# An embedding stage with four word buffers, normalized rows in PSUM and the text stores queued ahead of the expert weights' loads

## The chip, the cores and the metric

The kernel runs on one core of a Trainium2 chip. The metric is the device time of one execution in microseconds (us). TensorE (PE), VectorE (DVE), ScalarE (ACT), GpSimd (POOL) and SyncE (SP, which only issues transfers here) run side by side; each takes its instructions in order, and they wait for one another and for the DMA transfers by semaphores.

## What is computed

An early-fusion transformer block of depth 1, in float32. 64 images of 3 x 64 x 64 become 16 patches each, and 64 texts of 77 tokens become 77 rows each; together 64 x 93 = 5952 tokens of width 192. Attention and a product-key expert layer follow, with a residual around each.

```
tok:  patches(x) @ W.T + b                                 # 64 x 16 rows of 192
txt:  e = W_word[x_txt] + W_pos[pos] + W_type[..] + W_match_tok[..] + W_match_ent[..]
          + W_sf_tok[..] + W_sf_ent[..] + W_etype[..] + W_atype_ent[..]
      (e - mean(e)) * rsqrt(var(e) + 1e-12) * gamma + beta # 64 x 77 rows of 192
h = concat(tok, txt)                                       # per sample 93 rows
attn: w = h' @ w_qkv; softmax over the tokens of |w|^2 per head; out @ w_out + b_out
ffn:  z = x @ P; scores = z . C; top 4 of 64 in each of 8 groups;
      gelu(z W1[i]) W2[i] for the chosen ones, weighted; gelu(comb G1) G2
```

The change touches only the first two (`tok` and `txt`) and when the expert weights W2 are loaded.

## The kernel before

**Three stages.** The embedding stage writes all 5952 rows to a scratch tensor in DRAM (`h0`). The attention stage takes 16 units of 4 samples, and loads each unit's rows from it (`x0`). The expert stage takes 12 tiles of 496 tokens and holds nearly all of the time. One SBUF tensor (`arena`) is carved up anew for each stage, so the attention stage's tiles lie on the embedding stage's. `stage1_over` is the wait that separates them: all text and image stores landed (`s_todma`, `s_idma`), the three bfloat16 parts of w1 made (`s_ws`), b2 and w2 placed in their padded tiles (`s_bc`, `s_w2c`). Every engine executes it.

**Text rows.** The 4928 text rows are taken in 11 groups (`JJ`), each four tiles of 112 rows (16 samples x 7 positions). For group jj:

- GpSimd (`gather`) waits until the sum of group jj-2 is taken (`s_emb`), copies four columns of word ids to `wnow`, waits for the copy, and issues four indirect DMAs that fetch 112 rows of `W_word` each into `word[:, par]`, one of two buffers.
- VectorE (`onehots`) makes one-hot matrices of the position ids and the small tables' ids; TensorE (`tables`) multiplies them with the tables: 16 matmuls into PSUM (`pair0` or `pair1`).
- VectorE (`text_step(jj)`), in this order: one-hots of group jj+1; the sum of PSUM and word rows (`emb`, line 1166); `scaled(jj-1)` (line 1140); the statistics of jj (1173); `shifted(jj-1)` (1148), which adds beta and writes `tout`, one of two output buffers, after the stores of jj-3 have landed; moments of jj (1179) and the negated mean (1182).
- GpSimd (`text_rstd`, lines 691 and 693) makes the reciprocal deviation, ScalarE (`mean_off`, line 861) takes the mean off: from `emb` to `tnorm`, two SBUF buffers. `scaled` multiplies `tnorm` with deviation and gamma into `tmul`, in SBUF.
- SP (`store_text`, line 538) issues four stores of 16 x 7 rows each.

**Image rows.** TensorE (`image(k)`, 8 times 14 matmuls, lines 1515 and 1517) works on the patches `xt`, a load of 3 MB, into PSUM banks 4 and 5. ScalarE copies and stores them. In TensorE's order, tables of groups 0 and 1 come first, then twice `image` and once `tables`, four times, and the tables of groups 6 to 10 last.

**Expert weights.** W2 is loaded by 32 DMAs of 32 KB (line 549) into `w2f`, which lies on the patches' tile; so they wait for the last image matmul (`s_ips`). On SP they stand between `store_text(2)` and `store_text(3)`. W1 comes in one load of 1 MB that ScalarE issues (line 889) behind group 3. ScalarE casts it behind `mean_off(7)`; VectorE makes the rest (lines 1202 and 1205) between groups 8 and 9. ScalarE copies w2 to its place (line 905) behind `mean_off(8)`, and issues DMAs of the w1 parts (`stack_part`, line 873, 512 KB each) behind `mean_off` of groups 8, 9 and 10.

## Time and profile before

| | |
|---|---|
| median of 3 runs | 1409.76 us (1407.14 to 1412.56) |
| the profiled execution's own time | 1408.9 us |
| its span | 1406.8 us |
| busy, share of the span | PE 88%, DVE 78%, ACT 78%, POOL 72% |
| chain that ended last, first lines | ACT L1068 19%, ACT L1080 9%, POOL L821 5%, PE L1741 5%, PE L1728 4%, DVE L1476 4% |
| bytes moved | 107.05 MB |

The span is that of the instructions in the trace; 2.1 us lie around it. The chain's lines are those of the expert tiles (gelu, gates, the two products of each expert). The row format is: engine, line, operation, output<-input, and after it in brackets the idle time of the engine just before, with what ended it. "SPq" and "ACTq" are rows for DMA issues. An idle time that names a DMA ended when that transfer landed; where the engine named had long been done, it was another that came last.

### The profile page before, as it was taken

How to read it: one execution, taken by the hardware profiler on the slowest of the kernel's cores; microseconds unless marked ns; L12 is line 12 of the kernel's file. 1: busy time of each engine (PE TensorE's matmuls, PEld its weight loads, DVE VectorE, ACT ScalarE, POOL GpSimd, SP SyncE). 2: the span in 40 equal slices, each digit the busy share in tenths (PEclk: the TensorE clock that was granted, in tenths of full speed). 3: DMA queues.
4: the chain of work that ended last, by engine and by line, in shares of the span. 5: the costliest groups of instructions: out<-in, count | busy, mean ns of one | idle time of the engine just before them, and what ended most of it. 6: DMA issues, size and time to landing. Idle time of an engine off the chain costs nothing.

```text
span 1406.8 us, 34237 instructions
## 1 busy us (share of the span) xinstructions
PE 1237.8 (88%) x12232; PEld 622.3 (44%) x12232; DVE 1101.4 (78%) x3359; ACT 1093.7 (78%) x2708; POOL 1015.5 (72%) x735
## 2 busy tenths in 40 slices
PE   4742799999999999858999999999999999999996
PEld 3741466666666666533333333333333333333332
DVE  5574378888888888866888888888878888888883
ACT  0232557677767776538999999999999999999994
POOL 6661356775677567626888988888798888879894
PEclk8965799999999999968999999999999999999997
DMA  9644312322232222133224232222413322231410
GB/s 273 141 113 85 63 33 73 99 65 68 74 98 65 68 74 89 55 84 102 55 52 94 56 78 63 56 68 55 100 38 81 75 59 64 56 87 44 91 38 12
DMA packets 95704, 107.05 MB, mean 76 GB/s; under 512 B 12772, under 2 KB 92668, under 8 KB 95254
## 3 DMA queue, kind: packets, MB, share of 16 engines
q1 hardware_dynamic: 91184, 96.00, 26.5%
q10 hardware_dynamic: 2240, 5.08, 2.2%
q0 software_dynamic: 2112, 3.79, 1.1%
q8 instruction: 98, 1.61, 0.5%
q14 instruction: 70, 0.57, 0.1%
HBM read 67.88 MB, written 33.71 MB: 72 GB/s over the span
## 4 chain that ended last, share of the span: by engine, by line
ACT 29%; PE 11%; POOL 7%; DVE 4%; issue 4%; POOLq 0%; DVEq 0%; ACTq 0%
ACT ring L1068 19%; ACT arena L1080 9%; POOL arena L821 5%; PE code L1741 5%; PE ring L1728 4%; DVE arena L1476 4%; PE ring L1760 2%; POOL arena L829 1%; POOL arena L827 1%; ACT arena L1076 0%; ACT arena L1088 0%; PE ring L1751 0%; POOLq L157 0%; PE ring L1578 0%; PE ring L1626 0%
## 5 line engine op out<-in xcount | busy, mean ns | idle before, releaser
L1476 DVE TENSOR_TENSOR arena<-ring,arena 128x496 f32<-128x496 f32 x1008 | 611.6, 668 | 132.6 <-ACT ring L1068 131.8
L821 POOL TENSOR_TENSOR arena<-arena 128x992 f32<-128x992 f32 x264 | 608.4, 2316 | 113.5 <-ACT arena L1080 103.5
L1068 ACT ACTIVATE ring<-ring 128x496 f32<-128x496 f32 x1008 | 543.8, 689 | 11.8 <-PE ring L1728 10.8
L1728 PE MATMUL ring<-arena,w_stack 99*32 99x496 bf16 x6144 | 428.2, 375 | 25.6 <-DVE arena L1476 19.7
L1741 PE MATMUL code<-arena,w_pad 128*32 128x496 f32 x3072 | 389.0, 580 | 3.6 <-ACT arena L1084 3.3
L1728 PEld LDWEIGHTS ring<-arena,w_stack 99*32 99x32 bf16 x6144 | 159.8, 95 | 414.6 <-DVE arena L1476 252.4
L1080 ACT ACTIVATE arena<-ring 128x992 f32<-128x992 f32 x252 | 282.6, 1121 | 3.5 <-POOL arena L821 2.9
L1570 PE MATMUL ring<-arena 96*128 96x372 f32 x384 | 135.3, 490 | 1.6 <-ACT arena L924 0.9
L1741 PEld LDWEIGHTS code<-arena,w_pad 128*32 128x32 f32 x3072 | 96.6, 110 | 53.4 <-DVE arena L1476 17.8
L757 POOL TENSOR_TENSOR arena<-arena 128x372 f32<-128x372 f32 x96 | 91.9, 986 | 33.2 <-DVE arena L1316 33.2
L1570 PEld LDWEIGHTS ring<-arena 96*128 96x128 f32 x384 | 71.8, 194 | 62.4 <-ACT arena L932 15.8
L1619 PE MATMUL ring<-arena 128*128 128x376 f32 x192 | 78.5, 534 | 21.4 <-DVE arena L1311 15.3
L932 ACT ACTIVATE arena<-ring 128x93 f32<-128x93 f32 x384 | 92.6, 280 | 0.0
L752 POOL TENSOR_TENSOR arena<-arena 124x512 f32<-124x512 f32 x48 | 51.9, 1082 | 50.9 <-DVE arena L1248 50.7
L932 ACT ACTIVATION_READ_ACCUMULATOR arena<-ring 128x1 f32 x384 | 86.5, 239 | 0.0
L1248 DVE MAX8 arena<-arena 124x8 f32<-124x64 f32 x384 | 53.1, 211 | 40.8 <-ACT arena L969 40.8
L770 POOL TENSOR_TENSOR arena<-arena 124x576 f32<-124x576 f32 x16 | 22.4, 1402 | 82.5 <-DVE arena L1372 81.8
L1259 DVE MATCH_REPLACE8 arena<-arena 124x72 f32<-124x72 f32 x384 | 78.3, 216 | 0.0
L765 POOL TENSOR_TENSOR arena<-arena 128x372 f32<-128x372 f32 x96 | 74.7, 807 | 2.1 <-DVE arena L1338 2.1
L930 ACT COPY arena<-ring 128x372 f32<-128x372 f32 x96 | 46.9, 488 | 33.5 <-PE ring L1570 33.5
L1638 PE MATMUL code<-arena 128*124 128x192 f32 x384 | 68.9, 330 | 2.8 <-POOL arena L765 2.8
L918 ACT ACTIVATE arena<-arena 124x192 f32<-124x192 f32 x96 | 45.6, 539 | 33.1 <-DVE arena L1241 33.1
(140 smaller groups left out, 1467.1 us busy)
## 6 DMA issues: line engine op xcount, KB each, us to landing
arena<-gates SPq DMA_DIRECT2D x48, 496.0 KB, 6.7
gates<-arena SPq DMA_DIRECT2D x16, 744.0 KB, 11.5
arena<-h_scratch SPq DMA_DIRECT2D x32, 279.0 KB
arena<-z_parts SPq DMA_DIRECT2D x144, 62.0 KB, 2.7
h_scratch<-arena SPq DMA_DIRECT2D x16, 279.0 KB
z_parts<-arena SPq DMA_DIRECT2D x48, 93.0 KB, 2.1
arena<-h_scratch SPq DMA_DIRECT2D x12, 372.0 KB
out_h<-arena SPq DMA_DIRECT2D x12, 372.0 KB
```

The source lines that it names most:

```text
L757: p_.tensor_tensor(w2pi[:, c], wpi[:, c], wv[:, c], ALU.mult).then_inc(s_w2pi, 1)
L765: p_.tensor_tensor(o, o, natt[:, c].unsqueeze(2).to_broadcast([128, UB, N]), ALU.mult).then_inc(s_o, 1)
L821: p_.tensor_tensor(spaces[quad % SPACES][:, j:j + 2], hid[:, POOL_DUOS.index(duo) % 2], gst[:, block // EB, j:j + 2], ALU.mult).then_inc(s ...
L932: last = a_.activation(wsq[:, c, N * b:N * b + N], src[:, N * b:N * b + N], ACT.Square, accum_out=n2[:, c, b:b + 1])
L1068: a_.activation(product, product, ACT.Gelu_apprx_tanh).then_inc(s_hid, 1)
L1080: a_.activation(to_pool, product, ACT.Gelu_apprx_tanh).then_inc(s_hid, 1)
L1259: last = v_.match_replace(mr[:, s, g], v4[:, s, g], sc[:, s, g], CHOSEN)
L1476: v_.tensor_tensor(spaces[quad % SPACES][:, j + p], duo_bank(duo, p), gst[:, block // EB, j + p], ALU.mult).then_inc(s_gat, 1)
L1570: mm = t_.matmul(o, wq[:, h, 128 * c:128 * c + 128], xT["A"][:, h], start=(h == 0), stop=(h == 1))
L1619: t_.matmul(pair0[:, c % 2, 0:UB * (N + 1)], headsel[:, c], pis.rearrange("p b n -> p (b n)"), start=True, stop=True).then_inc(s_pb, 1)
L1728: mm = t_.matmul(bank[32 * q:32 * q + 32], w1s[:, x + 32 * q:x + 32 * q + 32], zst[:, o, j + p], start=True, stop=True)
L1741: mm = t_.matmul(code_bank[32 * j:32 * j + 32, 0:TN], w2p[:, chunk(2 * j + o, eb, k)], spaces[quad % SPACES][:, j], start=(quad == 0), sto ...
```

## The change

**Words.** There are four word buffers (`word_even`, and `word_odd` in a part of `arena` that the attention stage's small tiles leave free), each with a semaphore. `gather(jj)` waits for the sum of group jj-4 only, and reads its row ids from `widx` itself: `wnow` and its copy are gone. Groups 0 to 3 are gathered at the start.

**Rows in PSUM.** `mean_off` writes to PSUM banks 4 and 5 (`normed`), `scaled` works there in place, `shifted` reads from there. `tnorm` and `tmul` are gone. The row buffer is single: `mean_off(jj)` waits for `shifted(jj-1)`. Images use banks 6 and `code` in place of 4 and 5.

**SP's order.** Stores of groups 0 to 5 come first, then four times eight w2 loads and one group's stores, then the stores of group 10. The first `x0` load waits for stores alone (`stage1_stored`), and what is behind it for the whole of `stage1_over`.

**ScalarE's order.** w2 is placed behind `mean_off(10)`.

The core of the diff:

```diff
+        cw = Carver(cl.at)
+        word_odd = cw(TT, [2, 4, D])
...
+        def word(jj):
+            return (word_even, word_odd)[jj % 2][:, jj // 2 % 2]
+        def normed(rows=TT):
+            return ring[0:rows, 4:6, 0:2 * D]
...
-        def stage1_over(eng):
+        def stage1_stored(eng):
             eng.wait_ge(s_todma[0], 64 * 6)
             eng.wait_ge(s_todma[1], 64 * 5)
             eng.wait_ge(s_idma[0], 16 * 4)
             eng.wait_ge(s_idma[1], 16 * 4)
+        def stage1_over(eng):
+            stage1_stored(eng)
             eng.wait_ge(s_ws, 2)
...
-            store_text(0, 0)
-            store_text(1, 1)
-            store_text(2, 0)
+            for jj in range(6):
+                store_text(jj, jj % 2)
             sp.wait_ge(s_ips, 8)
...
-            for a in range(2):
-                for e in range(EB):
-                    for g in range(EB):
+            for e in range(EB):
+                for a in range(2):
+                    for g in range(EB // 2):
                         rows = slice(64 * a + 16 * e, 64 * a + 16 * e + 16)
-                        sp.dma_start(w2f[rows, g], w2_from[a, e, g]).then_inc(s_w2f, 16)
-            for pr in range(0, 4):
-                store_text(2 * pr + 3, 1)
-                store_text(2 * pr + 4, 0)
-            stage1_over(sp)
+                        sp.dma_start(w2f[rows, 2 * g], w2_from[a, e, 2 * g]).then_inc(s_w2f, 16)
+                        sp.dma_start(w2f[rows, 2 * g + 1], w2_from[a, e, 2 * g + 1]).then_inc(s_w2f, 16)
+                store_text(6 + e, e % 2)
+            store_text(10, 0)
+            stage1_stored(sp)
...
-            for i in range(-2, UNITS + 1):
+            pass_sp(-2)
+            stage1_over(sp)
+            for i in range(-1, UNITS + 1):
                 pass_sp(i)
...
-            def gather(jj, par):
-                wait_apart(pool, (s_emb, jj - 1))
-
-                p_.tensor_copy(wnow[:, par], widx[:, bass.ds(4 * jj, 4)]).then_inc(s_wnow, 1)
-                wait_apart(pool, (s_wnow, jj + 1))
+            def gather(jj):
+                wait(pool, s_emb, jj - 3)
                 for bb in range(4):
+                    x = 4 * jj + bb
                     p_.indirect_dma_start(
-                        word[:, par, bb], None, t["w_word"],
-                        bass.IndirectOffsetOnAxis(ap=wnow[:, par, bb:bb + 1], axis=0)).then_inc(s_word[par], 16)
+                        word(jj)[:, bb], None, t["w_word"],
+                        bass.IndirectOffsetOnAxis(ap=widx[:, x:x + 1], axis=0)).then_inc(s_word[jj % 4], 16)
...
-                a_.copy(img[:, k % 2], banks[k % 2][:, 0:D]).then_inc(s_iev, 1)
+                a_.copy(img[:, k % 2], banks[2 + k % 2][:, 0:D]).then_inc(s_iev, 1)
...
-                wait(act, s_tmul, jj - 1)
+                wait(act, s_to, jj)
                 for bb in range(4):
-                    last = a_.activation(tnorm[:, jj % 2, bb], emb[:, jj % 2, D * bb:D * bb + D], ACT.Identity,
+                    out = normed()[:, bb // 2, D * (bb % 2):D * (bb % 2) + D]
+                    last = a_.activation(out, emb[:, jj % 2, D * bb:D * bb + D], ACT.Identity,
                                          bias=tneg[:, bb:bb + 1])
...
-                if jj == 8:
+                if jj == 10:
                     act.wait_ge(s_w2f, 16 * 2 * EB * EB)
...
-                    last = v_.scalar_tensor_tensor(out=tmul[:, bb], in0=tnorm[:, par, bb], scalar=trs[:, bb:bb + 1],
+                    x = normed()[:, bb // 2, D * (bb % 2):D * (bb % 2) + D]
+                    last = v_.scalar_tensor_tensor(out=x, in0=x, scalar=trs[:, bb:bb + 1],
                                                    in1=tgam, op0=ALU.mult, op1=ALU.mult)
```

GpSimd's order at the start of the program, where L685 is a gather, L682 the copy of ids, and L691 with L693 `text_rstd`. Before:

```order
L682 COPY arena<-arena 112x4 [waits word_ids_loaded]
L685 DMA arena<-in_w_word,arena 112x192 [waits word_indices_placed]
L685 DMA arena<-in_w_word,arena 112x192 x3
L682 COPY arena<-arena 112x4
L685 DMA arena<-in_w_word,arena 112x192 [waits word_indices_placed]
L685 DMA arena<-in_w_word,arena 112x192 x3
L699 AFFINE_SELECT ident<-ident 128x128 [waits constants_zeroed]
L691 TENSOR_SCALAR arena<-arena 112x4 [waits text_moments]
L693 TENSOR_TENSOR arena<-arena 112x4 [waits text_var_eps]
L682 COPY arena<-arena 112x4 [waits emb_summed]
L685 DMA arena<-in_w_word,arena 112x192 [waits word_indices_placed]
```

And now, where L697 is a gather, L703 with L705 `text_rstd`:

```order
L697 DMA arena<-in_w_word,arena 112x192 [waits word_ids_loaded]
L697 DMA arena<-in_w_word,arena 112x192 x15
L711 AFFINE_SELECT ident<-ident 128x128 [waits constants_zeroed]
L703 TENSOR_SCALAR arena<-arena 112x4 [waits text_moments]
L705 TENSOR_TENSOR arena<-arena 112x4 [waits text_var_eps]
L697 DMA arena<-in_w_word,arena 112x192 [waits emb_summed]
```

Sixteen gathers stand ahead of the first `text_rstd` where eight stood.

SP's order from the stores of group 2 on, where L538 is a text store and L549 a w2 load. Before:

```order
L538 DMA h_scratch<-arena 16x7x192 [waits text_ready]
L538 DMA h_scratch<-arena 16x7x192 x3
L549 DMA arena<-in_w 16x8x64 [waits image_summed]
L549 DMA arena<-in_w 16x8x64 x31
L538 DMA h_scratch<-arena 16x7x192 [waits text_ready]
L538 DMA h_scratch<-arena 16x7x192 x3
```

And now from the stores of group 5 on, where L551 is a text store and L561 and L562 are w2 loads:

```order
L551 DMA h_scratch<-arena 16x7x192 [waits text_ready]
L551 DMA h_scratch<-arena 16x7x192 x3
L561 DMA arena<-in_w 16x8x64 [waits image_summed]
L562 DMA arena<-in_w 16x8x64
L561 DMA arena<-in_w 16x8x64
L562 DMA arena<-in_w 16x8x64
L561 DMA arena<-in_w 16x8x64
L562 DMA arena<-in_w 16x8x64
L561 DMA arena<-in_w 16x8x64
L562 DMA arena<-in_w 16x8x64
L551 DMA h_scratch<-arena 16x7x192 [waits text_ready]
L551 DMA h_scratch<-arena 16x7x192 x3
```

The one run of 32 loads behind three groups' stores is now four runs of 8, the first behind six groups' stores.

## Rows read from the trace of the kernel before

**Rows 1.** Windows of 4 us: busy time by engine, PEclk, DMA share, GB/s.

```profile
24.00:28.00 4.00, 0.00 (x0) 0.00 (x0) 3.97 (x16) 0.00 (x0) 3.41 (x3) 0.50 1.07 355
```

**Rows 2.** Timeline of SP, then VectorE, at the stage's end: start us, us, what.

```profile
114.39 7.76 SPq L538 DMA_DIRECT2D h_scratch<-arena  x8
...
123.75 0.27 SPq L557 DMA_DIRECT2D arena<-h_scratch  x1
...
117.86 0.96 DVE L1148 TENSOR_TENSOR arena<-arena 112x768 f32<-112x768 f32 x1
...
119.34 2.27 DVE L1213 TENSOR_TENSOR arena<-arena 128x2048 bf16<-128x2048 f32 x1
...
129.63 0.88 DVE L1228 BATCH_NORM_STATS2 arena<-arena 124x6 f32<-124x192 f32 x3 [5.00 <-DMA arena<-h_scratch]
```

**Rows 3.** Timeline of VectorE over one group, that of 3.

```profile
45.19 0.45 DVE L1130 TENSOR_SCALAR arena<-arena 128x448 f32<-128x448 int32 x1
...
49.38 0.94 DVE L1148 TENSOR_TENSOR arena<-arena 112x768 f32<-112x768 f32 x1
...
50.73 0.45 DVE L1130 TENSOR_SCALAR arena<-arena 128x448 f32<-128x448 int32 x1
```

**Rows 4.** Timeline of VectorE, embedding stage: waits in brackets, and the rest of w1.

```profile
38.41 0.96 DVE L1166 TENSOR_TENSOR arena<-ring,arena 112x768 f32<-112x768 f32 x1 [9.70 <-PE ring L1525]
...
67.82 0.96 DVE L1166 TENSOR_TENSOR arena<-ring,arena 112x768 f32<-112x768 f32 x1 [7.68 <-DMA arena<-in_w_word,arena]
...
81.56 0.96 DVE L1148 TENSOR_TENSOR arena<-arena 112x768 f32<-112x768 f32 x1 [4.87 <-DMA h_scratch<-arena]
...
96.87 1.06 DVE L1202 TENSOR_TENSOR arena<-arena 32x512 f32<-32x512 f32 x1
...
101.80 0.43 DVE L1130 TENSOR_SCALAR arena<-arena 128x448 f32<-128x448 int32 x1
...
110.18 0.96 DVE L1166 TENSOR_TENSOR arena<-ring,arena 112x768 f32<-112x768 f32 x1 [3.00 <-DMA arena<-in_w_word,arena]
```

**Rows 5.** Timeline of TensorE, embedding stage.

```profile
28.71 4.21 PE L1515 MATMUL ring<-arena 128*128 128x192 f32 x12 [12.80 <-DMA arena<-in_x]
...
52.18 0.49 PE L1525 MATMUL ring<-arena 128*112 128x192 f32 x2
...
59.33 0.49 PE L1525 MATMUL ring<-arena 128*112 128x192 f32 x2
...
107.27 0.85 PE L1525 MATMUL ring<-arena 128*112 128x192 f32 x2
```

**Rows 6.** Timeline of GpSimd: two groups' copy and gathers.

```profile
46.88 0.18 POOL L682 COPY arena<-arena 112x4 int32<-112x4 int32 x1
...
47.34 1.08 POOL L685 DMA_INDIRECT arena<-in_w_word,arena  x1 [0.28 <-POOL arena L682]
...
52.55 0.26 POOL L691 TENSOR_SCALAR arena<-arena 112x4 f32<-112x4 f32 x1
...
53.92 0.18 POOL L682 COPY arena<-arena 112x4 int32<-112x4 int32 x1
...
99.77 0.18 POOL L682 COPY arena<-arena 112x4 int32<-112x4 int32 x1
...
107.53 0.26 POOL L691 TENSOR_SCALAR arena<-arena 112x4 f32<-112x4 f32 x1
```

**Rows 7.** Timeline of SP; then the DMA queues, 0 to 150 us.

```profile
44.81 2.45 SPq L538 DMA_DIRECT2D h_scratch<-arena  x4
...
57.25 20.00 SPq L549 DMA_DIRECT2D arena<-in_w  x32
...
q0 software_dynamic: 2112, 3.79, 10.4%
```

**Rows 8.** Groups of instructions of VectorE, whole span, by shape.

```profile
L1357 DVE TENSOR_SCALAR arena<-ring,arena 128x93 f32<-128x93 f32 x16 | 4.8, 303 | 4.6 <-PE ring L1607 4.6
...
L1294 DVE TENSOR_SCALAR arena<-arena 128x93 f32<-128x93 f32 x16 | 4.3, 270 | 0.6
```

More of the change, by code:

```diff
@@ L222, in build @@
         widx = c1(TT, [JJ * 4], I32)
-        wnow = c1(TT, [2, 4], I32)
         pos_ids = c1(128, [B * NT], I32)
         small_ids = c1(SMALL, [B * NT], I32)
-        word = c1(TT, [2, 4, D])
+        word_even = c1(TT, [2, 4, D])
         ohp = c1(128, [2, 4, TT])
@@ L364, in build @@
         s_tneg, s_xm = sem("means_negated"), sem("mean_taken_off")
-        s_word = [sem("words_gathered0"), sem("words_gathered1")]
+        s_word = [sem(f"words_gathered{q}") for q in range(4)]
         s_oh, s_tps, s_emb, s_tst = sem("onehots_made"), sem("table_rows_summed"), sem("emb_summed"), sem("text_stats")
@@ L695, in _ @@
             pool.wait_ge(s_ix, 16)
-            gather(0, 0)
-            gather(1, 1)
+            for jj in range(4):
+                gather(jj)
             pool.wait_ge(s_zero, 1)
@@ L701, in _ @@
             text_rstd(0)
-            gather(2, 0)
+            gather(4)
             p_.affine_select(out=maskh, in_=maskh, compare_op=ALU.is_ge, fill=0.0, base=0,
@@ L709, in _ @@
             text_rstd(1)
-            gather(3, 1)
+            gather(5)
             for b in range(UB):
@@ L716, in _ @@
                                  pattern=[[-2, CH], [-1, 2], [0, DH]], channel_multiplier=1).then_inc(s_c2, 1)
-            text_rstd(2)
-            gather(4, 0)
-            for pr in range(0, 3):
-                for k in range(2):
-                    jj = 2 * pr + 3 + k
-                    text_rstd(jj)
-                    gather(jj + 2, 1 - k)
-            text_rstd(9)
-            text_rstd(10)
+            for jj in range(2, JJ):
+                text_rstd(jj)
+                if jj + 4 < JJ:
+                    gather(jj + 4)
             stage1_over(pool)
@@ L1147, in shifted @@
                 wait(dve, s_todma[par], use_count(jj, par))
-                v_.tensor_tensor(tout[:, par], tmul, tbet.unsqueeze(1).to_broadcast([TT, 4, D]),
+                v_.tensor_tensor(tout[:, par].rearrange("p (a b) d -> p a b d", a=2),
+                                 normed().rearrange("p a (b d) -> p a b d", b=2),
+                                 tbet.unsqueeze(1).unsqueeze(1).to_broadcast([TT, 2, 2, D]),
                                  ALU.add).then_inc(s_to, 1)
@@ L1161, in text_step @@
                 dve.wait_ge(s_tps, jj + 1)
-                if isinstance(jj, int):
-                    dve.wait_ge(s_word[par], 64 * (jj // 2 + 1))
-                else:
-                    dve.wait_ge(s_word[par], 32 * (jj - par) + 64)
+                dve.wait_ge(s_word[jj % 4], 64 * (jj // 4 + 1))
                 v_.tensor_tensor(emb[:, par].rearrange("p (a b) -> p a b", a=2),
                                  (pair0, pair1)[par][0:TT, :, 0:2 * D],
-                                 word[:, par].rearrange("p (a b) d -> p a (b d)", a=2), ALU.add).then_inc(s_emb, 1)
+                                 word(jj).rearrange("p (a b) d -> p a (b d)", a=2), ALU.add).then_inc(s_emb, 1)
                 if old:
@@ L1514, in image @@
                 for c in range(KC):
-                    t_.matmul(banks[k % 2][:, 0:D], xt[:, c, 128 * k:128 * k + 128], wtok[:, c],
+                    t_.matmul(banks[2 + k % 2][:, 0:D], xt[:, c, 128 * k:128 * k + 128], wtok[:, c],
                               start=(c == 0), stop=False)
-                t_.matmul(banks[k % 2][:, 0:D], ones_row, tokb, start=False, stop=True).then_inc(s_ips, 1)
+                t_.matmul(banks[2 + k % 2][:, 0:D], ones_row, tokb, start=False, stop=True).then_inc(s_ips, 1)
             def tables(jj, par):
```

3 lines of the change are left out of this document (removed).

## The prediction

> **What bounds the kernel now.** The profiled execution took 1408.9 us for a span of 1406.8, and the lines that its chain names first are those of the expert tiles, which the change does not touch. So the question is when the attention stage can begin. The embedding stage ends where SP issues the first load of `x0`, at 123.75 [rows 2]; that load waits for every text and image store, and reaches VectorE at 129.63. I take the 1283 us behind 123.75 as unchanged and cost the stretch in front of it.
>
> First the end of the stage, in the timelines of SP and VectorE. The last `shifted`, that of group 10, runs from 117.86 to 118.82, and its rows are stored at 123.75, 4.93 us later [rows 2]. The rest of the w1 parts ends at 121.61 (119.34 + 2.27), so it was not last [rows 2].
>
> Then VectorE's timeline backwards from there. An undisturbed group is one period from one-hots to one-hots, 45.19 to 50.73, 5.54 us [rows 3]. Eleven of them would take 61 us and the stage takes twice that, so I looked for its waits. Four matter [rows 4]: 9.70 us before the sum of group 2 (TensorE's tables, which stand behind the patches), 7.68 before that of group 5 (gathered words), 4.87 before `shifted` of group 5 (stores that stand behind the w2 loads), 3.00 before the sum of group 10 (words again). VectorE, fed late, is the chain.
>
> Last, what feeds it. TensorE starts on the patches at 28.71 and is done with the tables of group 5 at 59.82 (59.33 + 0.49) [rows 5]. GpSimd takes 7.04 us from one group's index copy to the next one's, 46.88 to 53.92, against VectorE's 5.54 [rows 6]. SP issues 32 w2 loads from 57.25 to 77.25 [rows 7], with the stores of group 3 and later queued behind them.
>
> **The change, part by part.**
>
> *Four word buffers, no index copy.* 16 gathers are issued before GpSimd waits for a sum. From then on a gather goes out four groups ahead of its sum instead of two, so the waits of 7.68 and 3.00 us on words go. GpSimd also loses 11 copies; a copy with the wait for it is 0.46 us (46.88 to 47.34), so its step becomes 7.04 - 0.46 = 6.58 [rows 6].
>
> The price: the gathers of groups 2 and 3, eight, now go out ahead of the time at which the patches land. The DMA engines are full there (share 1.07 from 24 to 28 us [rows 1]). The software queue's 44 gathers took 10.4% of 16 engines over 150 us [rows 7], so one is 150 x 0.104 / 44 = 0.355 us of all engines, and eight hold the patches up by at most 2.8 us; by nothing, at least, if the engines had room. I take 2.0, nearer the upper end because they were full.
>
> GpSimd also comes later to `text_rstd(0)`: four gathers are 5.2 us (47.34 to 52.55), so eight more are 10.4, some of it in time that was idle. VectorE has the 9.70 us of idle time before group 2 [rows 4] to hide what is left. Without that cover it would cost up to the 10.4.
>
> *Stores ahead of the w2 loads.* The stores of groups 3 to 5 no longer wait for 20 us of loads, and the wait of 4.87 goes. Behind `store_text(5)` SP now has 32 loads and 20 stores to issue: the check below.
>
> *Rows in PSUM.* Per group four ACTIVATEs write PSUM, four SCALAR_TENSOR_TENSORs read and write it, one TENSOR_TENSOR reads it. The row buffer is a single one, but `mean_off(jj)` waits for `shifted(jj-1)`, which stands in VectorE's order ahead of the negated mean that it waits for anyway: nothing. The nearest rows for the access: a TENSOR_SCALAR of 93 columns out of PSUM took 303 ns, out of SBUF 270 [rows 8], 33 ns more. On five VectorE instructions that is 0.17 us a group, 1.0 us over the last six groups. No row shows VectorE writing PSUM. Lower bound nothing; upper bound four times the row, 0.13 us an instruction, 4 us in all. I take 1.0, since the row is the same engine and access. (The Trainium skill, VectorE: DVE Perf Modes, section on the TRN2 errata, gives 120 cycles fixed for a PSUM source and 58 for an SBUF one, about 65 ns at the clock that it names. It speaks against the change; by it the term would be about 2 us, and the row has half of it.)
>
> *w2 placement last on ScalarE, images in other banks.* The copies leave the middle of the stage for its end. Their cover is the flight of `x0`, 123.75 to 129.63, 5.9 us. No cost; without the cover they would be some us on the path.
>
> *x0 as soon as the stores are in.* The waits taken from it ended at 121.61 or before, 2.1 us ahead of the stores. Worth nothing by itself, but it keeps the late w2 placement off the path.
>
> **The sum.** `emb(jj)` is the sum of group jj.
> - `emb(5)`: its tables done at 59.82, plus 2.0 for the patches: 61.8 (before 67.82 [rows 4]).
> - Five steps to `emb(10)`: 5 x 5.54 = 27.7, to 89.5. TensorE stays inside a step even at its slower pace, 0.85 us for two matmuls where 0.49 stood: the one-hots of group 10 began at 101.80 [rows 4] and its tables were done at 108.12 [rows 5], 6.3 us, a step and the 0.7 of the one-hots.
> - VectorE's rest of w1 between groups 8 and 9, 96.87 to 101.80, 4.9 [rows 4]: 94.4.
> - GpSimd: tables of group 4 done at 52.67 [rows 5], with the 2.0 at 54.7; moments a step without one-hots later, 4.8; `text_rstd(4)` 1.4 (52.55 to 53.92 [rows 6]): 60.9. Three steps of 6.58 on, `text_rstd(7)` is done at 80.6. VectorE wants it behind the sum of group 8, at 61.8 + 3 x 5.54 + 0.9 = 79.3. Wait 1.3: 95.7.
> - From the sum of group 10 to the end of `shifted`, 110.18 to 118.82, 8.6: 104.3.
> - PSUM access 1.0: 105.3.
> - Stores 4.9: 110.2.
>
> 123.75 - 110.2 = 13.5 us, so 1408.9 - 13.5 = 1395.4. The median of the three runs is 0.9 above the profiled execution: 1396.
>
> SP's check: `shifted(5)` ends 5.1 us behind the one-hots in whose step it stands (45.19 to 50.32 [rows 3]); these begin 0.7 ahead of `emb(6)` at 67.3, so it ends at 71.7. Four stores take 2.45 us to issue and a load 20.00 / 32 = 0.625 [rows 7]: 71.7 + 5 x 2.45 + 20.0 = 104.0, against 105.3 when the last rows are ready. SP is in time by 1.3 us only.
>
> **The rivals.** Times are on the median's footing, 1409.8.
> - *SP becomes the bound* (0.13). At 0.9 us a load the 32 end 8.8 later, the stage ends at 112.8 + 4.9 = 117.7 and the gain is 6: 1404. For it: the loads now share the engines with gathers, stores and the stack parts. Against: then they came in one run right behind the w1 load, now in four runs of eight with stores between. From 1.3 us of lateness on it decides.
> - *GpSimd becomes the bound* (0.08). The gathers of group 10 took 99.77 to 107.53, 7.76, beside VectorE's rest of w1 [rows 4, 6]. Less 0.46, with 1.4 for the rstd, a step of 8.7, 2.1 more than mine; on five steps 10. Gain 3.5: 1406. Against: that was one group of those shown, another took 5.7 (46.88 to 52.55).
> - *More comes back* (0.10). Patches not late, no dearer PSUM, GpSimd in time: 2.0 + 1.0 + 1.3 more, a gain of 17 to 20 with faster stores: 1391. (The Trainium skill, SBUF — State Buffer, section on the two separate sides, has a VectorE instruction with two SBUF inputs shut out a GpSimd one that reads SBUF. With rows in PSUM five instructions a group no longer have two. By that rule GpSimd's 1.3 us would go.)
> - *Slower* (0.05): VectorE's `scaled` and `shifted` on PSUM, the first with PSUM as output. Six groups of five are 30 instructions; at 0.48 us more each the gain is gone, at 0.7 it is 1416. Nothing near that size stands in rows 8.
> - *Nothing moves* (0.04): the patches alone hold the stage, and the waits for words and stores turn into others of the same size: 1409. Against it: each removed wait stands on VectorE's own timeline.
> - My forecast, a gain of 10 to 17 us: 0.60.
>
> **How the numbers follow.** A measurement of this kernel can tell about 0.5%, 7 us, from no change. Faster by more: 0.60, 0.10, half of SP's 0.13 and a third of GpSimd's: 0.79. Slower: 0.05. Between: 0.16. The range 1389 to 1403 leaves out the slower case, no change and the worse halves of the first two rivals, under 2 in 10.
>
> **What would show it.** In the profile after: the patches' first matmul at 29 to 31.5; `emb(5)` at 60 to 63 without a wait for words; no wait of VectorE for stores; steps of 5.5 to 6.6; `x0` issued near 110; `scaled` as long as before to 0.1 us an instruction. I am wrong if SP begins its last stores later than `shifted(10)` ends, if the gathers stretch, if the patches come more than 3 us late, or if the span behind the `x0` load is other than 1283 us.

## The result and the profile after

| kernel | median | runs | ratio to before, 95% interval |
|---|---|---|---|
| before | 1408.51 us (1406.86 to 1412.56) | 6 | |
| after | 1399.42 us (1398.49 to 1401.25) | 6 | 0.9932 (0.9919 to 0.9946) |

The kernel became faster by 9.1 us, 0.7%. The forecast was 1396, with a range of 1389 to 1403. The profiled execution of the changed kernel took 1400.24 us for a span of 1398.2; before it was 1408.9 for 1406.8.

The page's first part after, busy time and instructions by engine:

```profile
PE 1236.3 (88%) x12232; PEld 622.2 (44%) x12232; DVE 1099.5 (79%) x3359; ACT 1093.8 (78%) x2708; POOL 1007.3 (72%) x724
```

The shares say nothing here, since 1283 us of the span are not concerned. What answers to [rows 2] is the stage's end. Timeline of SP after (start us, us, what), from the last run of w2 loads to the first `x0` load. L561 and L562 are w2 loads, L551 text stores, L569 the `x0` load:

```profile
94.95 3.88 SPq L551 DMA_DIRECT2D h_scratch<-arena  x4
98.87 0.59 SPq L561 DMA_DIRECT2D arena<-in_w  x1
99.50 1.39 SPq L562 DMA_DIRECT2D arena<-in_w  x1
...
102.48 1.45 SPq L562 DMA_DIRECT2D arena<-in_w  x1
...
104.48 0.43 SPq L562 DMA_DIRECT2D arena<-in_w  x1
104.95 5.78 SPq L551 DMA_DIRECT2D h_scratch<-arena  x8
112.32 10.32 SPq L569 DMA_DIRECT2D arena<-h_scratch  x2
```

`x0` is loaded at 112.32, where it was 123.75 [rows 2]: 11.4 us earlier. Now VectorE's timeline after, which answers to [rows 3, 4]. L1174 is the sum of a group (`emb`), L1149 `scaled`, L1157 `shifted`, L1213 the rest of w1:

```profile
40.32 0.96 DVE L1174 TENSOR_TENSOR arena<-ring,arena 112x768 f32<-112x768 f32 x1 [9.08 <-PE ring L1533]
...
61.77 0.96 DVE L1174 TENSOR_TENSOR arena<-ring,arena 112x768 f32<-112x768 f32 x1 [1.79 <-PE ring L1533]
...
67.17 0.94 DVE L1174 TENSOR_TENSOR arena<-ring,arena 112x768 f32<-112x768 f32 x1
...
72.69 0.94 DVE L1174 TENSOR_TENSOR arena<-ring,arena 112x768 f32<-112x768 f32 x1
74.73 1.40 DVE L1149 SCALAR_TENSOR_TENSOR ring<-ring,arena 112x192 f32<-112x192 f32 x4 [1.10 <-POOL arena L705]
...
86.15 3.98 DVE L1213 TENSOR_TENSOR arena<-arena 128x512 f32<-128x512 f32 x4
...
96.41 0.96 DVE L1174 TENSOR_TENSOR arena<-ring,arena 112x768 f32<-112x768 f32 x1 [0.99 <-PE ring L1533]
...
104.03 0.96 DVE L1157 TENSOR_TENSOR arena<-ring,arena 112x768 f32<-112x768 f32 x1
...
117.94 0.88 DVE L1236 BATCH_NORM_STATS2 arena<-arena 124x6 f32<-124x192 f32 x3 [4.34 <-DMA arena<-h_scratch]
```

The waits of 7.68 and 3.00 us for gathered words and of 4.87 for stores [rows 4] are gone. What is left in the brackets is TensorE up to group 5 (9.08, then three times 1.79), after it 0.16, 1.10 and 1.10 for GpSimd, and in group 10 0.99 for TensorE and 1.52 for ScalarE. The last `shifted` ends at 104.99 where it ended at 118.82 [rows 2]: 13.8 us earlier. So 2.4 of the 13.8 us that VectorE gained were lost again between VectorE's end and the `x0` load. That interval is 7.33 us now and was 4.93.

TensorE's timeline after, the patches, which answers to the first row of [rows 5]:

```profile
30.91 4.17 PE L1523 MATMUL ring<-arena 128*128 128x192 f32 x12 [14.20 <-DMA arena<-in_x]
```

Behind the `x0` load stand 1285.9 us, not 1283.05, 2.8 us more. So of 11.4 us at the load 8.6 reach the span. Whether the change costs these 2.8 us is one of the questions below.

### The profile page after: what moved, and what is told of

Read it like the earlier page. It is cut to its first block, busy times and chain, and to the rows that moved or that the text cites. A ratio compares the mean times of both kernels' runs of the same rounds, so it can differ in the third digit from the quotient of the medians.

```text
span 1398.2 us, 34230 instructions
## 1 busy us (share of the span) xinstructions
PE 1236.3 (88%) x12232; PEld 622.2 (44%) x12232; DVE 1099.5 (79%) x3359; ACT 1093.8 (78%) x2708; POOL 1007.3 (72%) x724
## 3 DMA queue, kind: packets, MB, share of 16 engines
q0 software_dynamic: 2112, 3.79, 1.0%
## 4 chain that ended last, share of the span: by engine, by line
ACT 28%; PE 11%; POOL 7%; DVE 4%; issue 4%; SPq 1%; DMA 0%; POOLq 0%; DVEq 0%; ACTq 0%
ACT ring L1076 18%; ACT arena L1088 9%; POOL arena L828 5%; PE code L1749 5%; PE ring L1736 5%; DVE arena L1484 4%; PE ring L1768 2%; POOL arena L836 1%; POOL arena L834 1%; ACT arena L1084 0%; DMA bias_codes<-arena 0%; ACT arena L1096 0%; SPq L618 0%; PE ring L1759 0%; SPq L623 0%
## 5 line engine op out<-in xcount | busy, mean ns | idle before, releaser
L1627 PE MATMUL ring<-arena 128*128 128x376 f32 x192 | 78.5, 534 | 24.2 <-DVE arena L1319 16.0
L1267 DVE MATCH_REPLACE8 arena<-arena 124x72 f32<-124x72 f32 x384 | 78.4, 217 | 0.0
L772 POOL TENSOR_TENSOR arena<-arena 128x372 f32<-128x372 f32 x96 | 74.7, 807 | 2.1 <-DVE arena L1346 2.1
L1646 PEld LDWEIGHTS code<-arena 128*124 128x124 f32 x384 | 65.1, 193 | 7.2 <-POOL arena L772 3.4
```

What stands on the lines that cost most here:

```text
L1267: last = v_.match_replace(mr[:, s, g], v4[:, s, g], sc[:, s, g], CHOSEN)
L1627: t_.matmul(pair0[:, c % 2, 0:UB * (N + 1)], headsel[:, c], pis.rearrange("p b n -> p (b n)"), start=True, stop=True).then_inc(s_pb, 1)
L1646: last = t_.matmul(o, wpi[:, c, ST * s:ST * s + ST], wout[:, c], start=(c == 0), stop=(c == CH - 1))
```

## The experiments

In the traces the patches land anywhere between 28.7 and 35.5 us with their load at the same place. To compare kernels across chips I therefore read the stretch from the first image matmul (`img`) to the first `x0` load, and the tail behind that load. "End to x0" is from the end of group 10's `shifted` to the load. All are worked out from the starts in each kernel's timelines.

| kernel | img | x0 | img to x0 | end to x0 | tail |
|---|---|---|---|---|---|
| before | 28.71 | 123.75 | 95.0 | 4.9 | 1283.1 |
| before2 | 30.00 | 125.59 | 95.6 | 5.0 | 1282.1 |
| words | 34.30 | 124.45 | 90.2 | 5.0 | 1284.8 |
| stores | 31.87 | 122.23 | 90.4 | 6.7 | 1285.1 |
| rows_sbuf | 35.48 | 118.23 | 82.8 | 7.8 | 1280.2 |
| after | 30.91 | 112.32 | 81.4 | 7.3 | 1285.9 |
| after2 | 31.59 | 113.37 | 81.8 | 7.8 | 1282.1 |
| after3 | 30.96 | 113.61 | 82.7 | 7.9 | 1282.4 |
| x0_with_all | 33.30 | 115.29 | 82.0 | 7.7 | 1283.6 |
| spread | 33.32 | 111.80 | 78.5 | 5.0 | 1279.6 |
| spread3 | 31.82 | 110.26 | 78.4 | 5.0 | 1285.6 |
| spread3b | 32.54 | 111.98 | 79.4 | 5.0 | 1281.1 |
| patches_first | 22.61 | 113.46 | 90.9 | 4.9 | 1281.5 |

My theory after the result: the gain is that of the waits for words and for stores taken away together, and what fell short is SP, which comes late with the stores of groups 9 and 10. Rivals: one of the two edits does it all; rows in PSUM cost or give time; the early gathers hold up the patches; the split of the `x0` wait is worth something.

### words: the four word buffers alone

The kernel before, with this alone:

```diff
-            def gather(jj, par):
-                wait_apart(pool, (s_emb, jj - 1))
-
-                p_.tensor_copy(wnow[:, par], widx[:, bass.ds(4 * jj, 4)]).then_inc(s_wnow, 1)
-                wait_apart(pool, (s_wnow, jj + 1))
+            def gather(jj):
+                wait(pool, s_emb, jj - 3)
```

> The kernel before with the words' part alone: four buffers, no index copy. SP still issues the 32 w2 loads in one run ahead of store 3, rows stay in SBUF. Theory A (the two removed waits lie in series, and the run of loads holds the stores whatever the words do): the sum of group 5 comes at about 62 us instead of 67.8, but shifted of group 5 still waits for the stores of group 3, until about 83; only the waits on words of groups 8 and 10 go, so x0 is issued at 119 to 121.5, 2 to 5 us earlier than 123.75. Rival B (words are most of the gain): x0 at 114 to 117.

Measured: 1408.15 us (1405.55 to 1412.28, 10 runs) against 1409.16 of the kernel before (21 runs), ratio 0.9996 (0.9982 to 1.0009). No change. VectorE's waits in its timeline, sums of groups 4 and 5, then `shifted` of group 5:

```profile
58.65 0.96 DVE L1159 TENSOR_TENSOR arena<-ring,arena 112x768 f32<-112x768 f32 x1 [1.77 <-PE ring L1518]
65.80 0.96 DVE L1159 TENSOR_TENSOR arena<-ring,arena 112x768 f32<-112x768 f32 x1 [1.76 <-PE ring L1518]
...
85.55 0.96 DVE L1144 TENSOR_TENSOR arena<-arena 112x768 f32<-112x768 f32 x1 [10.52 <-DMA h_scratch<-arena]
```

No wait for words is left. But the wait for stores, 4.87 us before, is 10.52 now: VectorE came earlier to the same stores, which stand behind 32 w2 loads. From `img` to `x0` 5 us were gained, and in this trace `x0` is still issued at 124.45, not at 119 to 121.5, because the patches landed at 34.30. The ten runs show no gain either (at most 2.5 us by the interval). On the same chip the patches of `stores`, with the old eight gathers ahead of them, landed at 31.87; if the 16 gathers hold them up by those 2.4 us in every execution, half of the gain goes there. Where the rest of it goes, no run shows.

### stores: SP's order, the split `x0` wait and the w2 placement alone

The kernel before, with this alone, and with the w2 copies behind `mean_off(10)`:

```diff
-            store_text(0, 0)
-            store_text(1, 1)
-            store_text(2, 0)
+            for jj in range(6):
+                store_text(jj, jj % 2)
...
+                store_text(6 + e, e % 2)
+            store_text(10, 0)
+            stage1_stored(sp)
```

> The kernel before with SP's and ScalarE's order alone: stores of groups 0 to 5 first, then four times eight loads and one group's stores, w2 placed behind mean_off(10), x0 after stores. Two word buffers, rows in SBUF. Theory A: the wait for stores goes, and the gathers of group 5 no longer share the engines with the run of loads, so its sum comes at 62 to 63; then GpSimd's step of about 7.2 us, with gathers only two groups ahead, sets the pace; x0 at 114 to 117, a gain of 7 to 10. Rival B: without the word buffers the wait for words of group 5 stays at 5 us or more and x0 is issued at 118 or later.

Measured: 1404.37 us (1400.05 to 1409.41, 10 runs), ratio 0.9970 (0.9954 to 0.9986): 4.8 us by the medians, 2 to 6.5 by the interval. The sums of groups 4 and 5 in VectorE's timeline:

```profile
57.91 0.96 DVE L1170 TENSOR_TENSOR arena<-ring,arena 112x768 f32<-112x768 f32 x1 [3.31 <-DMA arena<-in_w_word,arena]
68.53 0.96 DVE L1170 TENSOR_TENSOR arena<-ring,arena 112x768 f32<-112x768 f32 x1 [5.19 <-DMA arena<-in_w_word,arena]
```

No wait for stores stands in that timeline, and the waits for words stay: 3.31, 5.19, and behind them 3.30, 2.13 and 1.64. So it was Rival B: the wait before group 5 stayed above 5 us, and `x0` came at 122.23, where Theory A had 114 to 117. From `img` to `x0` it is 90.4, as in `words`. Each edit alone takes about 5 us off that stretch; the two together, without the rows in PSUM, take 12 (`rows_sbuf`, next). By the medians on this chip it is 1.0 and 4.8 us alone and 9.3 together. The waits stand in series on one engine: taking one away lets VectorE run into the other.

### rows_sbuf: the changed kernel with the rows in SBUF again

```diff
-                wait(act, s_to, jj)
+                wait(act, s_tmul, jj - 1)
...
-                    out = normed()[:, bb // 2, D * (bb % 2):D * (bb % 2) + D]
-                    last = a_.activation(out, emb[:, jj % 2, D * bb:D * bb + D], ACT.Identity,
+                    last = a_.activation(tnorm[:, jj % 2, bb], emb[:, jj % 2, D * bb:D * bb + D], ACT.Identity,
...
-                    last = v_.scalar_tensor_tensor(out=x, in0=x, scalar=trs[:, bb:bb + 1],
+                    last = v_.scalar_tensor_tensor(out=tmul[:, bb], in0=tnorm[:, par, bb], scalar=trs[:, bb:bb + 1],
...
-                v_.tensor_tensor(tout[:, par].rearrange("p (a b) d -> p a b d", a=2),
-                                 normed().rearrange("p a (b d) -> p a b d", b=2),
-                                 tbet.unsqueeze(1).unsqueeze(1).to_broadcast([TT, 2, 2, D]),
+                v_.tensor_tensor(tout[:, par], tmul, tbet.unsqueeze(1).to_broadcast([TT, 4, D]),
```

> The changed kernel with the normalized rows in SBUF again (tnorm in two buffers, tmul). Theory A (place of the rows is worth nothing at the end, because SP ends last): median within 1 us of the changed kernel; shifted(10) may end up to 2 us later than 105.0. Rival B (VectorE with two SBUF inputs holds GpSimd up): gathers of 1.1 to 1.3 us mean instead of 0.97, GpSimd's step over 7 us, shifted(10) ends at 108 or later and x0 is issued 2 us or more later than 112.3. Rival C (PSUM access is dearer): shifted(10) ends about 1 us earlier.

Measured: 1399.86 us (1397.44 to 1404.99, 6 runs), ratio 0.9935 (0.9915 to 0.9956), by the time no different from the changed kernel. The trace tells more. Groups of instructions from 26 to 110 us (count, busy us, mean ns), of the changed kernel for GpSimd, VectorE and ScalarE:

```profile
L697 POOL DMA_INDIRECT arena<-in_w_word,arena x28 | 27.3, 976 | 7.8 <-issue 7.6 <-DVE arena L1174 0.2
L1149 DVE SCALAR_TENSOR_TENSOR ring<-ring,arena 112x192 f32<-112x192 f32 x44 | 15.4, 418 | 6.7 <-POOL arena L705 5.1 <-ACT ring L869 1.5
L869 ACT ACTIVATE ring<-arena 112x192 f32<-112x192 f32 x40 | 14.6, 410 | 27.1 <-DVE arena L1190 23.1 <-issue 2.5 <-ACT arena L860 1.4
```

And of `rows_sbuf`:

```profile
L699 POOL DMA_INDIRECT arena<-in_w_word,arena x28 | 31.8, 1137 | 7.8 <-issue 7.8
L1149 DVE SCALAR_TENSOR_TENSOR arena<-arena 112x192 f32<-112x192 f32 x44 | 15.6, 415 | 6.4 <-POOL arena L707 4.2 <-ACT arena L870 2.0
L870 ACT ACTIVATE arena<-arena 112x192 f32<-112x192 f32 x40 | 14.9, 443 | 28.1 <-DVE arena L1188 24.2 <-ACT arena L862 2.1 <-issue 1.8
```

`scaled`, with PSUM as input and output, takes 418 ns against 415: the access costs nothing. ScalarE writes PSUM 33 ns faster. The gathers are what differs, 976 against 1137 ns. Timelines of `rows_sbuf` show where, GpSimd first:

```profile
71.33 0.30 POOL L705 TENSOR_SCALAR arena<-arena 112x4 f32<-112x4 f32 x1
...
74.34 0.94 POOL L699 DMA_INDIRECT arena<-in_w_word,arena  x1 [0.30 <-issue]
75.58 1.63 POOL L699 DMA_INDIRECT arena<-in_w_word,arena  x1 [0.30 <-issue]
77.51 0.93 POOL L699 DMA_INDIRECT arena<-in_w_word,arena  x1 [0.30 <-issue]
78.46 0.26 POOL L705 TENSOR_SCALAR arena<-arena 112x4 f32<-112x4 f32 x1
```

and then VectorE, `shifted` beside the long one:

```profile
75.31 0.93 DVE L1157 TENSOR_TENSOR arena<-arena 112x768 f32<-112x768 f32 x1
```

From 26 us on, six gathers of `rows_sbuf` take 1.36 to 1.77 us and all six lie beside a `shifted` whose two inputs are in SBUF. In `words` it is five, 1.51 to 1.76. In the changed kernel and in `spread3`, where one input of `shifted` is in PSUM, no gather from 26 us on takes over 1.1. GpSimd's step, from one `text_rstd` to the next, is 7.13 us here (71.33 to 78.46). In the changed kernel it is 6.45. VectorE waits 1.65 us a group for it where it waits 1.10; all its waits for GpSimd behind group 5 are 3.77 us against 2.36. So the rows in PSUM help VectorE by way of GpSimd, 0.6 us a group that GpSimd limits, 1.4 us by those waits. From `img` to the end of the last `shifted` less of it is left: 74.9 us here, 74.0 to 74.7 in the changed kernel's three traces and in `x0_with_all`. That is less than the medians resolve. Of the expectations, Theory A's median held and so did Rival B's gathers and step; its later `x0` can't be told from patches that landed at 35.48.

(The Trainium skill, SBUF — State Buffer, section on the two separate sides, has a VectorE instruction with two SBUF inputs and a GpSimd instruction that reads SBUF shut each other out, and whichever starts first goes first; the traces agree for the 768 columns of `shifted`.)

The four shorter SCALAR_TENSOR_TENSORs of `scaled` have two SBUF inputs as well. In `rows_sbuf` they lengthen no gather from 26 us on by more than 0.04 us (1.11 or 1.12 for 1.08). In the kernel before they do, near the start of the stage; GpSimd's timeline, then VectorE's:

```profile
24.42 2.14 POOL L685 DMA_INDIRECT arena<-in_w_word,arena  x1 [0.28 <-POOL arena L682]
...
24.21 1.39 DVE L1140 SCALAR_TENSOR_TENSOR arena<-arena 112x192 f32<-112x192 f32 x4
```

From the end of the four `scaled`, 25.60, to the end of this gather, 26.56, are 0.96 us, a gather's ordinary time.

### before2 and after2: the same two kernels on one chip

> The kernel before, unchanged, traced a second time beside the changed one on the same chip. Theory A (16 early gathers hold the patches up): its first image matmul begins 1.5 to 3 us earlier than that of after2. Rival B (when the patches land is a matter of chip and run): no earlier, or within 1 us. The last unit's interval between h1 stores is either near 25.2 or near 28.0 us, by chance.

> The changed kernel, unchanged, traced a second time. Theory A: from the first image matmul to the x0 load 81.4 us again, within 1 (95.0 in the kernel before); from the x0 load to the end of the span anything between 1279.5 and 1286, in steps that TensorE's clock makes in the first and the last unit. Rival B (the 2.8 us lost behind x0 belong to the change): near 1286 again.

Measured: before2 one run, 1409.76 us (the kernel before beside it 1408.08, 11 runs). after2 1399.43 us (1397.52 to 1402.82, 6 runs), ratio 0.9936 (0.9916 to 0.9956). The patches' first matmul, before2, in TensorE's timeline:

```profile
30.00 4.21 PE L1515 MATMUL ring<-arena 128*128 128x192 f32 x12 [14.72 <-DMA arena<-in_x]
```

and after2:

```profile
31.59 4.07 PE L1523 MATMUL ring<-arena 128*128 128x192 f32 x12 [16.13 <-DMA arena<-in_x]
```

On one chip the patches came 1.6 us later; the forecast had 2.0. It is one pair, and kernels that issue as many gathers differ by more. The chip of `words` and `stores` gives three more pairs: with eight gathers ahead the patches landed at 31.87 (`stores`), with 16 at 33.32 (`spread`), 34.30 (`words`) and 35.48 (`rows_sbuf`). Each time the kernel with eight was first. From `img` to `x0` it was 81.8, within 1 of the 81.4 before. The tails here are 1282.1 and 1282.1, so Rival B is out: the change costs nothing behind the `x0` load. The 2.8 us of the first pair are something else. Windows of the last attention unit in the changed kernel's first trace (busy us by engine, then the granted clock, the DMA share and GB/s):

```profile
581.00:587.00 6.00, 3.21 (x13) 2.18 (x10) 5.90 (x46) 2.59 (x6) 5.17 (x7) 0.79 0.09 32
587.00:593.00 6.00, 6.00 (x27) 5.91 (x26) 5.11 (x28) 1.53 (x4) 2.47 (x2) 0.64 0.01 3
```

and in after2:

```profile
581.00:587.00 6.00, 3.20 (x18) 1.53 (x18) 5.86 (x46) 2.43 (x5) 5.97 (x8) 1.00 0.21 66
587.00:593.00 6.00, 5.99 (x41) 5.75 (x39) 5.87 (x30) 2.05 (x5) 2.46 (x2) 1.00 0.01 2
```

1.00 is 2.4 GHz and 0.50 would be 1.2; a value between is the mean over a window that had both. Of the same program, in the same place, one execution had a granted clock of 0.79 and 0.64 and the other the full one; in the window before, 575 to 581 us, both had 1.00 with TensorE busy for 4.76 of 6 us. The interval between the last two stores of attention units is 28.0 us in the first and 25.5 in the second, and over all thirteen traces it is 25.2 to 28.0. In the kernel before it was 25.2, so this unit accounts for the 2.8 us of the first pair. It is not the only place: `spread3` has 25.2 here and a tail of 1285.6 all the same. What decides it in a given execution, no run here shows.

### spread: SP begins its w2 loads two groups earlier

The changed kernel, with stores of groups 0 to 3 first, then four times eight loads and one group's stores, and those of groups 8 to 10 last:

```diff
-            for jj in range(6):
+            for jj in range(4):
                 store_text(jj, jj % 2)
...
-                store_text(6 + e, e % 2)
-            store_text(10, 0)
+                store_text(4 + e, e % 2)
+            for jj in range(8, JJ):
+                store_text(jj, jj % 2)
             stage1_stored(sp)
```

> The changed kernel with the w2 loads begun earlier: eight loads behind each of the stores of groups 3, 4, 5 and 6. Theory A (SP's queue, not VectorE, set the end of the stage by about 2 us): SP is idle when shifted(10) ends near 105, the stores of group 10 are issued at once, x0 at about 110, 2 to 2.5 us earlier than 112.3. Rival B (the engines, full with the third stack part and the loads, set it): x0 no earlier than 111.5. From x0 to the end of the span: 1283 if the 2.8 us lost behind the stage are chance of one run, 1286 if they belong to the changed kernels.

Measured: 1398.46 us (1393.44 to 1399.92, 4 runs), ratio 0.9926 (0.9906 to 0.9947). SP's timeline at the end:

```profile
85.81 4.87 SPq L561 DMA_DIRECT2D arena<-in_w  x8
90.72 19.47 SPq L551 DMA_DIRECT2D h_scratch<-arena  x16
111.80 10.32 SPq L569 DMA_DIRECT2D arena<-h_scratch  x2
```

All loads are out at 90.7, and the last `shifted`, which ends at 106.8, is followed by the `x0` load 5.0 us later, as in the kernel before. From `img` to `x0` it is 78.5 us, 3 to 4 less than in the changed kernel. By its time alone `x0` at 111.80 would fit Rival B, 111.5 or later; but the patches landed at 33.32, 2.4 us later than in the first trace, and SP stood idle when the last `shifted` ended, which is Theory A. That settles SP's part, in the trace; in the medians of these few runs the two cannot be told apart.

### spread3 and spread3b: the same, with the gathers three groups ahead

A test of the early gathers: 12 instead of 16 stand ahead of the first `text_rstd`.

```diff
-            for jj in range(4):
+            for jj in range(3):
                 gather(jj)
...
-                if jj + 4 < JJ:
-                    gather(jj + 4)
+                if jj + 3 < JJ:
+                    gather(jj + 3)
```

> The kernel spread (w2 loads behind the stores of groups 3 to 6) with gathers three groups ahead in place of four: 12 gathers before anything waits. Theory A (each early gather delays the patches by 0.2 to 0.36 us): first image matmul about 1 us earlier than in after2; no wait for words; from there to x0 78.5 us as in spread; time 2.5 to 4 us below after2. Rival B (three ahead is too short): waits for words on VectorE return, x0 no earlier than in spread.

> spread3, a second trace and five more rounds on the chip of after3. Theory A: 78.4 us from the first image matmul to the x0 load, x0 2.5 to 3.5 us earlier than in after3, time 2 to 3.5 us below it. Rival B (the gain at x0 is eaten behind it): within 1 us of after3.

Measured: 1397.67 us (1395.73 to 1401.72, 6 runs), ratio 0.9917 (0.9897 to 0.9938), and on another chip 1394.60 (1392.72 to 1397.04, 5 runs), ratio 0.9900 (0.9884 to 0.9917). From `img` to `x0` 78.4 and 79.4, as in `spread`, and no wait for words: a fourth buffer isn't needed. The patches landed at 31.82 and 32.54. With 16 gathers on the same chips it was 31.59 and 30.96 (33.30 in `x0_with_all`), so twelve gathers brought them no earlier, against Theory A, and what each gather costs the patches stays open. This is the fastest version that I ran: over both labels the median of 11 runs is 1395.9, over the three labels of the changed kernel that of 18 runs is 1399.8. The changed kernel beside them is 1.8 us slower on the one chip, where the intervals overlap, and 6.2 us on the other, where no run of the two overlaps; the forecasts were 2.5 to 4 and 2 to 3.5. So that something is gained is shown on one chip, and its size is anywhere between these two. Two edits stand in it, SP's order and the gathers; `spread` gives the whole of the stretch with SP's order alone.

### patches_first: the patches ahead of the late ids

`spread3`, with the loads of patches and their weights issued ahead of those of the ids of groups 2 and later:

```diff
-            sp.dma_start(small_ids[:, late], t["small_ids"][:, late]).then_inc(s_tl, 16)
...
             sp.dma_start(xt, t["x"].rearrange("(c p) n -> p c n", p=128)).then_inc(s_xt, 16)
+            sp.dma_start(small_ids[:, late], t["small_ids"][:, late]).then_inc(s_tl, 16)
```

> spread3 with the patches' loads (tok_w, tok_b, x) issued ahead of the late small and position ids (2.4 MB). Theory A (the patches' landing heads the chain): first image matmul 4 to 6 us earlier than in spread3, but GpSimd, with gathers, masks and the head selector still to do, then holds groups 2 and 3; x0 2 to 4 us earlier than in spread3. Rival B (GpSimd takes all of it, or the one-hots of group 2 wait for the ids as long as the patches did): x0 within 1 us of spread3.

Measured: 1398.03 us (1397.06 to 1401.75, 6 runs), ratio 0.9924 (0.9905 to 0.9943), no gain over `spread3` beside it. VectorE's timeline, the late position ids, then `scaled` of two groups:

```profile
32.69 2.25 DVE L1129 TENSOR_SCALAR arena<-arena 2x4032 int32<-2x4032 int32 x1 [16.05 <-DMA arena<-in_pos_ids]
...
52.73 1.40 DVE L1149 SCALAR_TENSOR_TENSOR ring<-ring,arena 112x192 f32<-112x192 f32 x4 [3.20 <-POOL arena L705]
...
59.21 1.40 DVE L1149 SCALAR_TENSOR_TENSOR ring<-ring,arena 112x192 f32<-112x192 f32 x4 [1.11 <-POOL arena L705]
```

The image matmuls began at 22.61, some 9 us earlier, and nothing was gained: now VectorE waits 16.05 us for the ids that landed late instead, and from 52.73 on GpSimd sets the pace, 6.48 us a group (52.73 to 59.21), with a wait of 1.11 in each. `x0` came at 113.46, 3.2 us later than in `spread3`, where the one theory had 2 to 4 earlier and the other no difference; both of the causes that the rival named are in the trace.

### x0_with_all and after3: the split of the `x0` wait

```diff
             store_text(10, 0)
-            stage1_stored(sp)
+            stage1_over(sp)
```

> The changed kernel with the first x0 load behind the whole of stage1_over again. Theory A: the stores land within 0.3 us of the end of w2's placement (112.3 and 112.5 in the first trace), so x0 is issued 0 to 1 us later and the time is that of after3 within 1 us. Rival B (the placement, late behind the last loads, was kept off the path by the split): x0 2 us or more later, from the first image matmul 83.5 us or more in place of 81.6.

> The changed kernel, a third trace and five more rounds beside the others. From the first image matmul to the x0 load 81 to 82.5 us; behind the x0 load 1279.5 to 1286, whichever way TensorE's clock falls in the first and last unit.

Measured: 1400.91 us (1399.84 to 1401.75, 6 runs), ratio 0.9946 (0.9933 to 0.9959), and the changed kernel beside it 1400.81 (1398.05 to 1402.35, 6 runs), ratio 0.9948 (0.9935 to 0.9962). The split is worth nothing. In the changed kernel's ScalarE timeline the w2 placement is

```profile
109.95 2.55 ACT L913 COPY w_pad<-arena 128x256 f32<-128x256 f32 x8 [7.40 <-DMA arena<-in_w]
```

which ends at 112.50, 0.2 us behind the `x0` load at 112.32: the two waits end together. In `x0_with_all` the load is issued at 115.29, 7.7 us after the last `shifted`, as with the split (7.3 to 7.9). With SP's loads earlier, as in `spread`, I did not try it.

## Why the prediction was right, and where it was off

The measured 1399.4 us lie 3.4 above the forecast and inside its range. The chain that it described is the one that the traces show; one step came out late, the stores that SP issues last, and the terms for PSUM and for GpSimd are right only in their sum.

**What bounds the kernel: right.** Each of the three waits that the prediction read in [rows 4] was real time, but not one by one: taken alone, words and stores give 5 us each of the stretch from `img` to `x0`, together 12. Had only one of them been changed, the same reasoning (a wait of 7.68 and 3.00, hence 10 us) would have been wrong by half or more: the medians give 1.0 us for the words and 4.8 for the stores.

**The patches, +2.0:** 30.91 against 28.71, 1.6 on one chip, 1.5 to 3.6 on another. The size fits, and every pair has the sign. But the landing varies by as much from trace to trace, and twelve gathers in place of 16 brought nothing back, so that it is the gathers' own traffic is argued, not shown.

**`emb(5)` at 61.8:** 61.77.

**Five steps of 5.54, w1's rest 4.9:** 34.6 us from `emb(5)` to `emb(10)`, against 33.9. A step is 5.36 without its wait (67.17 to 72.69, less 0.16), 0.18 less than forecast, and w1's rest is 4.9. The last step was counted as a full one, but no one-hots stand in it; TensorE's tables then hold the sum of group 10 by 0.99, and the two cancel. What is left over is GpSimd's.

**GpSimd, a wait of 1.3:** 0.16 + 1.10 + 1.10 = 2.36. The forecast had `text_rstd(7)` done at 80.6 and it was at 81.09 (80.04 + 1.05), 0.5 late: the step of 6.58 came out as 6.45, but the first of the three was longer, since GpSimd waited for VectorE's moments in it. The other 0.5 is VectorE's, three steps shorter by 0.18.

**`text_rstd(0)` late, hidden:** right. VectorE waits 2.77 us for it at 26.74, and 9.08 for TensorE behind that.

**PSUM access, +1.0: next to nothing.** The `scaled` rows show 3 ns an instruction, and ScalarE's are 33 ns shorter. The nearest row that I took, with a [128 x 93] tile and 33 ns, does not carry over. (The Trainium skill, VectorE: DVE Perf Modes, section on the TRN2 errata, has a fixed cost of 120 cycles for a PSUM source and 58 for an SBUF one, by an estimate from its clock about 65 ns more; the 3 ns here, and the same 0.93 to 0.96 us for `shifted` with either source, do not agree.) What PSUM gives is in GpSimd's gathers, as the rival *more comes back* had it; but GpSimd's wait did not go, it was 2.36 us with the rows in PSUM.

**VectorE's end:** forecast 105.3, measured 104.99. That it is so near is in part luck: the 1.0 for PSUM that was not paid stands in for the 0.7 by which `emb(5)` to `emb(10)` was too short.

**SP's check: the step that failed.** `shifted(5)` ended at 71.57 (forecast 71.7) and the loads began at 74.09 as they should. Then the check had 20.0 us of loads and four groups' stores, 9.8, to 103.9. Measured: the four runs of loads took 3.9, 3.9, 5.0 and 6.0, together 18.9. The stores between and behind them took 2.85, 3.79, 3.88 and 3.2 us, 13.7, not 9.8. And SP stood 1.2 us idle ahead of the stores of group 8, which were not ready. So it came to the last four stores at 108.20, 3.2 us behind the rows, and issued these in 2.52, 0.8 less than in the kernel before (3.3): that leaves the 2.4 lost. The rival *SP becomes the bound* is thus what happened to the last step, at a third of its price: `x0` at 112.3, not 110.2, nor 117.7. The rival charged the loads, 0.9 us each. They took 0.59 on average, and the stores were what was dear. `spread` shows that 2.3 to 2.9 us come back when SP has no loads left there. SP's last four stores in the changed kernel:

```profile
108.20 2.52 SPq L551 DMA_DIRECT2D h_scratch<-arena  x4
```

The loads aren't what made the stores dear. The check took its 2.45 us from the stores of group 3, and the kernel before has others. Its SP and ScalarE timelines, stores of groups 7 and 8, then two of the four of group 8, where no w2 load is left (L873 issues a part of w1):

```profile
96.49 3.95 SPq L538 DMA_DIRECT2D h_scratch<-arena  x4
97.00 0.63 ACTq L873 DMA_DIRECT2D w_stack<-arena  x1
...
106.72 3.87 SPq L538 DMA_DIRECT2D h_scratch<-arena  x4
107.23 0.59 ACTq L873 DMA_DIRECT2D w_stack<-arena  x1
...
107.93 1.16 SPq L538 DMA_DIRECT2D h_scratch<-arena  x1
...
109.14 1.45 SPq L538 DMA_DIRECT2D h_scratch<-arena  x1
```

In most other rows a store takes 0.6 us. In all thirteen traces the two that SP begins 0.7 and 1.9 to 2.0 us after ScalarE begins to issue the second w1 part take 1.14 to 1.49. The parts were in the same place of ScalarE's order before, so the price stood in the trace that the prediction read: with 3.95, 3.87 and 3.79 us for three of its five groups of stores, the check gives 108.2 for the last four, as measured. That the w1 parts are the cause is argued from this timing; no run moved them.

**The tail unchanged: right, in the second pair.** 1282.1 on both sides; the 2.8 us in the first pair are those of the last attention unit, 28.0 us against 25.2, at a lower granted clock.

**The sum.** From `img` to `x0` the forecast was 110.2 - 30.7 = 79.5 us, against 81.4 to 82.7 in three traces. At the load 11.4 us were gained in the first pair and 12.2 in the second, forecast 13.5; by the medians of three comparisons it is 7.9 to 9.1. The second pair's profiled executions differ by 12.2 us too (1409.76 and 1397.52), and the changed kernel's executions there spread over 5 us. Why the medians give 2 to 4 us less than the traces is not settled; the tails alone differ by up to 6.3 us among the thirteen traces (1279.6 to 1285.9), and no run separates what causes that.

## What to carry to other kernels

Waits that one engine meets in series can be worth more together than the sum of each alone (9.3 us here, against 1.0 and 4.8): read which resource the engine would run into next before pricing a single one away, and try the edits together if each alone gives little. When transfers are queued on one issuing engine, count its whole queue up to the last store, at the prices that the trace has in that very stretch rather than the cheapest row of an earlier one, and put loads that nobody needs yet where the queue has slack. A landing that comes earlier is worth nothing if what was moved behind it is needed at the same time.

## What the runs showed of the hardware

- A gather issue of GpSimd, 112 rows of 768 bytes, takes 0.93 us with 0.30 between two. Beside a VectorE instruction with two inputs of 768 columns in SBUF it takes up to 1.77; with one of them in PSUM it stays at 0.93 to 1.08. Beside four of 192 columns with two SBUF inputs it took 2.14 at one place of the kernel before, and in `rows_sbuf` 1.12 at most. One gather of the changed kernel took 2.90, at 19.48, beside a VectorE instruction with a single SBUF input (2 x 4032 int32, 2.24 us at 20.02).
- VectorE with PSUM as input and output, 192 columns in f32: 418 ns, with SBUF for both 415. ScalarE writes 192 columns to PSUM in 410 ns and to SBUF in 443.
- SP issues a 32 KB load in 0.43 us in most rows, and in 1.39 and 1.45 at two places (99.50 and 102.48 in the changed kernel), 4.0 and 1.4 us after ScalarE issued a w1 part of 512 KB. Four stores take 2.45 us in the middle of the stage and mostly 3.2 to 3.95 in the 5 us behind ScalarE's issue of a w1 part, with w2 loads in the queue or without.
- The same program's last attention unit took 25.5 us in one execution and 28.0 in another, with a granted clock of 1.00 in the one and 0.64 to 0.79 in the other.
